# Two phases of a kernel in one program block: each engine goes on by single waits where all engines met

## The reference, cut to what matters

```
# phase A: layer norm, RWKV attention (16 heads, chunks), output projection, residual
out = rwkv(layernorm(x)) + x                     # x1
# phase B: layer norm, mixture of experts, residual
router_logits = h @ gate_w.T                     # h = layernorm(x1), 8 experts, 2 chosen per token
capacity = int(s * K / E * CAP_FACTOR)           # 320 rows at most for each expert and batch item
h1, h3 = dispatch @ w1[e], dispatch @ w3[e]      # 256 -> 896
expert_out = (silu(h1) * h3) @ w2[e]             # 896 -> 256
final = sum over chosen experts of prob * expert_out
```

## Time and profile before

| | us |
|---|---|
| median of 3 executions | 925.23 |
| lowest, highest | 925.21, 929.25 |
| the profiled execution | 925.3 |
| its span, first to last instruction | 923.2 |

### The profile page before, as it was taken

One profiled execution on the slowest core, in us unless ns is written; L12 is line 12 of the kernel. 1 busy time (PEld: TensorE's weight loads), 2 busy tenths in 40 slices (PEclk: granted clock), 3 DMA queues, 4 the chain that ended last, 5 costly groups with the idle time before them and its releaser, 6 DMA issues. The chain is left out here.

```text
span 923.2 us, 19140 instructions
## 1 busy us (share of the span) xinstructions
PE 851.7 (92%) x6919; PEld 724.0 (78%) x6920; DVE 490.8 (53%) x1207; ACT 462.5 (50%) x844; POOL 454.3 (49%) x496
## 2 busy tenths in 40 slices
PE   3999899999999999697999999999799999999995
PEld 2778777777777777687889889879689879889885
DVE  5887788888888876233442342442142343242330
ACT  3567666666666767154443452443253444353331
POOL 5445666666555666356237346237236136437024
PEclk9999999999999999799999999999899999999998
DMA  4840222212111122456024417025325214414113
GB/s 149 330 167 24 88 89 68 67 54 77 37 37 37 37 66 77 147 127 167 8 80 86 112 55 138 7 81 87 73 81 86 71 41 105 94 40 46 13 17 42
DMA packets 50470, 74.01 MB, mean 80 GB/s; under 512 B 5056, under 2 KB 42176, under 8 KB 50368
## 3 DMA queue, kind: packets, MB, share of 16 engines
q1 hardware_dynamic: 35488, 53.46, 17.7%
q0 software_dynamic: 14592, 19.18, 12.1%
q10 hardware_dynamic: 288, 0.01, 0.0%
HBM read 38.41 MB, written 34.22 MB: 79 GB/s over the span
## 5 line engine op out<-in xcount | busy, mean ns | idle before, releaser
L1540 POOL TENSOR_TENSOR wlo<-wraw,whi 128x448 fp32r<-128x448 f32 x84 | 102.6, 1225 | 213.3 <-ACT whi L1596 213.3
L1817 PE MATMUL p<-xh,whi 128*128 128x512 f32 (+1 forms) x504 | 191.7, 380 | 13.6 <-PEq L1446 5.6
L1733 DVE TENSOR_TENSOR hid<-gated,p 128x512 f32<-128x512 f32 (+1 forms) x126 | 81.1, 644 | 214.0 <-ACT gated L1610 214.0
L1819 PE MATMUL p<-xh,wlo 128*128 128x512 f32 (+1 forms) x504 | 190.8, 379 | 0.0
L1818 PE MATMUL p<-xl,whi 128*128 128x512 f32 (+1 forms) x504 | 190.4, 378 | 0.0
L1548 POOL DMA_INDIRECT out<-ysb,index x80 | 125.7, 1571 | 95.1 <-ACT ysb L1632 65.0
L1610 ACT ACTIVATE gated<-p 128x512 f32<-128x512 f32 (+1 forms) x126 | 71.0, 564 | 188.6 <-PE p L1819 188.6
L1837 PE MATMUL py<-whi,hh 128*128 128x256 f32 x469 | 135.6, 289 | 10.6 <-PEq L398 7.5
L1839 PE MATMUL py<-whi,hl 128*128 128x256 f32 x469 | 133.0, 284 | 0.0
L1838 PE MATMUL py<-wlo,hh 128*128 128x256 f32 x469 | 132.8, 283 | 0.0
L1817 PEld LDWEIGHTS p<-xh,whi 128*128 128x128 f32 x504 | 95.4, 189 | 34.3 <-issue 12.1
(11 more groups left out here) (197 smaller groups left out, 1434.1 us busy)
## 6 DMA issues: line engine op xcount, KB each, us to landing
wraw<-in_w SPq DMA_DIRECT2D x24, 896.0 KB
disp<-wraw SPq DMA_DIRECT2D x16, 662.5 KB, 8.8
xtok<-disp SPq DMA_DIRECT2D x16, 530.0 KB, 5.4
x_ring<-in_x SPq DMA_DIRECT2D x16, 256.0 KB, 3.8
out<-x SPq DMA_DIRECT2D x16, 256.0 KB
xtok<-disp SPq DMA_DIRECT2D x8, 265.0 KB, 6.8
out<-ysb,index POOLq DMA_INDIRECT x80
disp<-row,slot_i POOLq DMA_INDIRECT x64
```

Of the source, the lines that this page charges most:

```text
L1540: nc.gpsimd.tensor_tensor(wlo[e.const % 2][m][:, cut], wraw[k][:, cut], whi[e.const % 2][m][:, cut].bitcast(F32), ALU.subtract).then_inc(w ...
L1733: nc.vector.tensor_tensor(hid[k][:, 0:w], gated[k][:, 0:w], p3[k][:, 0:w], ALU.mult).then_inc(hid_ready, 1)
L1817: nc.tensor.matmul(dst[:, 0:w], hi[m][:, wcut], xh[xcut], start=(kt == 0), stop=False)
L1819: ins = nc.tensor.matmul(dst[:, 0:w], lo[m][:, wcut], xh[xcut], start=False, stop=(kt == KT - 1))
```

## The change

Each phase function now returns its five engine programs in place of running them in a block of its own, and `build` puts both in one block, phase A's before phase B's for each engine. Without the meeting, these waits hold what it held: GpSimd waits for the stores of x1 (`x1_out`) before its first add to `out`; TensorE and ScalarE wait for `taken_ready` before their first branch; SP's wait for `sent` before its loads was there already. The `ysb` buffers move to `Kept`, to memory that phase A doesn't use. The PSUM banks of phase B are named in another order, so that the banks of p1 and p3 are those which `early_up` fills, and py0, py1, pt0 and pt1 are banks that phase A is done with. In the diff below, lines that are only shifted to another indentation are left out.

```diff
@@ build @@
-            phase_a(nc, *tensors(ctx), ctx, sem, ident, x, maa, decay_row, decay_ch, u_row,
-                    (wrT, wkT, wvT, wgT, woT), lnw, lnb, gateT, disp, out, whi[0], wlo[0], wraw, expert_views(w1, w3, w2), taken, kept)
+            first = phase_a(nc, *tensors(ctx), ctx, sem, ident, x, maa, decay_row, decay_ch, u_row, (wrT, wkT, wvT, wgT, woT),
+                            lnw, lnb, gateT, disp, out, whi[0], wlo[0], wraw, expert_views(w1, w3, w2), taken, kept)
...
-            phase_b(nc, sb2, ps2, ctx, sem, ident, whi, wlo, wraw, w1, w2, w3, taken, disp, out, kept)
+            second = phase_b(nc, sb2, ps2, ctx, sem, ident, whi, wlo, wraw, w1, w2, w3, taken, disp, out, kept)
+            with nc.Block() as block:
+
+                @block.sync
+                def _(sp):
+                    first[0](sp)
+                    second[0](sp)
...
+                @block.tensor
+                def _(pe):
+                    first[4](pe)
+                    second[4](pe)
@@ class Kept @@
+        self.ysb = [sb(f"ysb{k}", [P, C]) for k in range(NY)]
@@ phase_a @@
-    with nc.Block() as block:
-
-        @block.sync
-        def _(sp):
+    def on_sync(sp):
...
+    return on_sync, on_gpsimd, on_scalar, on_vector, on_tensor
@@ phase_b @@
-    ysb = [sb(f"ysb{k}", [P, C]) for k in range(NY)]
+    ysb = kept.ysb
 
-    p1 = [ps(f"p1_{k}", [P, CW]) for k in range(2)]
-    p3 = [ps(f"p3_{k}", [P, CW]) for k in range(2)]
-    py = [ps(f"py{k}", [P, 512]) for k in range(2)]
-    pt = [ps(f"pt{k}", [P, 512]) for k in range(2)]
+    banks_in_order = {n: ps(n, [P, 512]) for n in ("py0", "p1_1", "p3_1", "p3_0", "pt0", "pt1", "py1", "p1_0")}
+    p1, p3, py, pt = [[banks_in_order[f"{n}{k}"] for k in range(2)] for n in ("p1_", "p3_", "py", "pt")]
...
+    taken_ready, x1_out = sem("taken_ready"), [sem(f"x1_out{k}") for k in range(2)]
@@ phase_b, GpSimd, first @@
             pool.wait_ge(index_early, 1)
+            for k in range(2):
+                pool.wait_ge(x1_out[k], 16 * STEPS // 2)
             early = tile_order(e)[:CHUNKS[EARLY][1]]
@@ phase_b, ScalarE, first @@
             scale_out(e, t0 + n - 1)
+            act.wait_ge(taken_ready, 1)
             rest_where_taken(e)
@@ phase_b, TensorE, first @@
             down(e, t0 + n - 1)
+            pe.wait_ge(taken_ready, 1)
             rest_where_taken(e)
```

More of the change, by code:

```diff
@@ L68 @@
 CW = max(n for _, n in CHUNKS) * P
+NY = 4
 EARLY = 1
@@ new lines, in across, with within @@
+                ins.then_inc(across_done, 1)
+        def within(b, t, g):
+            if 0 <= b < STEPS:
+                c, e = g // 2, g % 2
+                pe.wait_ge(attm_ready[g], TPS * b + t + 1)
+                for d in range(BANDS):
+                    ins = nc.tensor.matmul(pY[d * 2 * N:(d + 1) * 2 * N, c, t * Q:(t + 1) * Q],
+                                           v_pad[:, t, c * BANDS + d, e * 2:(e + 1) * 2, :].rearrange("p a n -> p (a n)"),
+                                           attm[g][:, d, :], start=False, stop=(t == TPS - 1 and g == HGS - 1 and d == BANDS - 1),
+                                           skip_group_check=True)
+                ins.then_inc(intra_done[g], 1)
@@ new lines, in group_sums @@
+        def group_sums(b):
+            if 0 <= b < STEPS:
+                pe.wait_ge(ysq_ready, b + 1)
+                wait(pe, x1_ready, b)
+                if b == 0:
+                    pe.wait_ge(set_pool, 2)
+                heads = blockdiag[:].rearrange("p (h n) -> p h n", n=N)[:, :, 0]
+                for t in range(TPS):
+                    for k in range(KT):
+                        ins = nc.tensor.matmul(p_sums[:, t, k * HPB:(k + 1) * HPB], ysq[:, k, t * Q:(t + 1) * Q], heads,
+                                               start=True, stop=True)
+                ins.then_inc(ssum_done, 1)
@@ new lines, in turn2, with logits @@
+        def turn2(b):
+            if 0 <= b < STEPS:
+                pe.wait_ge(xn2_ready, b + 1)
+                for t in range(TPS):
+                    for c in range(KT):
+                        ins = nc.tensor.transpose(p_x2[:, c, t * Q:(t + 1) * Q], row[b % 2][:, t, c * P:(c + 1) * P], ident[:])
+                ins.then_inc(x2t_done, 1)
+        def logits(b):
+            if 0 <= b < STEPS:
+                pe.wait_ge(x2T_ready, b + 1)
+                for t in range(TPS):
+                    for c in range(KT):
+                        ins = nc.tensor.matmul(p_logit[:, t, :], x2T[:, c, t * Q:(t + 1) * Q], gate_sb[:, c, :],
+                                               start=(c == 0), stop=(c == KT - 1))
+                ins.then_inc(logit_done, 1)
@@ new lines, in count @@
+        def count(b):
+            if 0 <= b < STEPS:
+                r = b % 2
+                n = TPS + (b % SPB == SPB - 1)
+                pe.wait_ge(took_ready, b + 1)
+                nc.tensor.matmul(pS[:, 1, 0, 0, 0:n * E], ones[:], before[r][:, 0:n, :].rearrange("p t e -> p (t e)"), start=True, stop=False)
+                nc.tensor.matmul(pS[:, 1, 0, 0, 0:TPS * E], tri[:], took[r][:].rearrange("p t e -> p (t e)"),
+                                 start=False, stop=True).then_inc(count_done, 1)
@@ new lines, in early_turn, with early_up @@
+        def early_turn(i):
+            pe.wait_ge(rows_in, 16)
+            if i == 0:
+                pe.wait_ge(state_ready, TPS * STEPS - 1)
+            else:
+                pe.wait_ge(gT_ready, STEPS)
+            for a in range(CHUNKS[EARLY][1]):
+                ins = nc.tensor.transpose(early_turned[i][:, a * P:(a + 1) * P],
+                                          kept.xtok[:, EARLY_T.start + a, i * P:(i + 1) * P], ident[:])
+            ins.then_inc(turned, 1)
+        def early_up(f):
+            if f == 0:
+                pe.wait_ge(xl_ready, KT)
+                pe.wait_ge(wlo_ready, 2 * WP)
+                pe.wait_ge(attm_ready[HGS - 1], TPS * STEPS)
+                pe.wait_ge(y_ready, STEPS)
+                pe.wait_ge(ysq_ready, STEPS)
+            wait(pe, hid_ready, f - 1)
+            for m, dst in ((0, early_p1[f % 2]), (1, early_p3[f % 2])):
+                for kt in range(KT):
+                    wcut = slice(kt * F + f * P, kt * F + (f + 1) * P)
+                    nc.tensor.matmul(dst, whi[m][:, wcut], kept.xh[:, kt, early_cols], start=(kt == 0), stop=False)
+                    nc.tensor.matmul(dst, whi[m][:, wcut], kept.xl[:, kt, early_cols], start=False, stop=False)
+                    ins = nc.tensor.matmul(dst, wlo[m][:, wcut], kept.xh[:, kt, early_cols], start=False, stop=(kt == KT - 1))
+            ins.then_inc(h_done, 1)
@@ new lines, in on_tensor @@
+        for c in range(-1, TAIL):
+            group_sums(c - 1)
+            across(c, 0)
+            scores_a(c)
+            outer(c)
+            turn1(c + 1)
+            project_g(c)
+            spread(c - 1)
+            within(c, 0, 0)
+            scores_b(c)
+            within(c, 0, 1)
+            within(c, 0, 2)
+            across(c, 1)
+            within(c, 0, 3)
+            project_r(c + 1)
+            project_k(c + 1)
+            for g in range(HGS):
+                within(c, 1, g)
+            count(c - 3)
+            turn2(c - 2)
+            project_o(c - 1)
+            logits(c - 2)
+            project_v(c + 1)
+            turn_k(c + 1)
@@ new lines, in on_tensor @@
+        group_sums(14)
+        across(15, 0)
+        scores_a(15)
+        outer(15)
+        project_g(15)
+        spread(14)
+        within(15, 0, 0)
+        scores_b(15)
+        within(15, 0, 1)
+        within(15, 0, 2)
+        across(15, 1)
+        within(15, 0, 3)
+        within(15, 1, 0)
+        within(15, 1, 1)
+        within(15, 1, 2)
+        within(15, 1, 3)
+        count(12)
+        early_turn(0)
+        early_turn(1)
+        turn2(13)
+        project_o(14)
+        logits(13)
@@ new lines, in on_sync, with load_rows, load_weights, step @@
+    def on_sync(sp):
+        def load_rows(e):
+            e.wait(sp, turned, TB)
+            e.wait(sp, rows_used, 2)
+            for k, (t0, n) in enumerate(ROW_LOADS):
+                if e.reg is None and e.const == 0 and k == 0:
+                    continue
+                src = (t0 - REST) % ST
+                sp.dma_start(xtok[:, t0:t0 + n, :], row_of(rows_view, e)[:, src:src + n, :]).then_inc(rows_in[k], 16)
+        def load_weights(e, m):
+            even, u = pair(e)
+            k = (3 * u + m) % 2
+            e.wait(sp, wlo_ready, 3 * WP, WP * (m - 1))
+            dst = wraw[k][:].rearrange("p (k f) -> p k f", k=KT if m < 2 else FT)
+            sp.dma_start(dst, row_of(w_view[m], e)).then_inc(w_in[k], 16)
+        for k in range(2):
+            sp.wait_ge(sent[k], 16 * TPS * 2 * STEPS // 2)
+        load_rows(At(0))
+        def step(e):
+            nxt = e + 1
+            if nxt.valid(E):
+                for m in range(2):
+                    load_weights(nxt, m)
+                load_rows(nxt)
```

(2 more changed lines are left out.)

2310 lines of the change are left out of this document (1085 added, 1225 removed).

## The result

The changed kernel takes 921.08 us in the median of 13 executions (918.99 to 927.49), the kernel before 926.13 us in 13 (925.21 to 929.77). The ratio is 0.9948, with a 95% interval of 0.9933 to 0.9964: 4.8 us less on 926, between 3.3 and 6.2. Measured again, on two other occasions, it was 0.9960 (0.9943 to 0.9977) and 0.9953 (0.9939 to 0.9967). The direction is clear; the size is at the 0.5% that I had called the line between faster and the same: the median is 0.5 us above that line, 920.6, and 0.08 us above the 921 beyond which I had called the forecast wrong as a whole.

A forecast was written before the change was run, and what follows sets the result against it. TensorE, busy 92% of the span, was taken as the bound, its wait at the phase join the largest reachable. 4.69 (earlier restart) + 1.06 (clock) = 5.75 us off 925.3 gave 919.5 us, range 917.0 to 924.5.

The forecast's parts named there:

- the forecast's own case: At the join, the clock falls and comes back soon, costing 0.8 to 2.7 us: 919.5 us, chance 0.47.
- the sign of 921: Whole program: the forecast is wrong as a whole if the median lies above 921 us.
- Step 1: At the join, TensorE restarts at 378.70 in place of 383.39, after VectorE's last hidden part: gain 4.69 us.
- Step 2: Behind the join, the clock falls once more, costing 1.5 us in place of 2.56: gain 1.06 us.
- Step 3: Behind the removed meeting, the waits put in its place are hidden and cost nothing.
- (a): At the join, SP's wait for `sent` ends 2.3 us behind the last scatter; rows land at 384.3, before TensorE's transposes.
- (b) to (e): Second phase: waits for `x1_out` and `taken_ready`, weight loads and casts, new banks and `ysb` place each cost nothing.
- The signs: Timeline checks: `down` 2.8 us behind `early_up`, released by `hl`; low clock behind; times from fourth tile 5.8 us earlier.
- Clock stays high: At the join, the clock does not fall: gain 7.25 us, 918.0 us; chance 0.26.
- No earlier start: At the join, TensorE gets little or no earlier start: 921 to 926 us; chance 0.16.
- One more stall at a branch: At a branch behind the join, moved code adds 5.0 us and 2.7 of low clock: 927.2 us; chance 0.07.

The follow-up runs named there:

- the late split: Changed kernel with the first two tiles of expert 0's last chunk begun early on the parts of hidden that are there; 918.55 us, 0.9899 to the kernel before.
- the filled kernels: Changed kernel plus 12 unused matmuls on TensorE filling the idle 2.8 us at the join; 922.03 us (0.9942), then 920.97 us (0.9936) to the kernel before.
- two blocks: Changed kernel with two blocks and the meeting between them restored, its other parts kept; 905.6 us, 1.0002 to the kernel before.

## Why the prediction was right, and where not

The forecast of 919.5 us lay 1.6 us below the median of 921.08, and the range, 917.0 to 924.5, held it. The narrower range of the forecast's own case, 918.8 to 920.8, did not, nor did the sign of 921. Some 0.8 us of the miss is the start: the kernel before took 926.13 us over 13 executions and not 925.3. The rest is a gain of 5.05 us in place of 5.75, and the term that was mis-sized is the clock. By its steps:

**Step 1, the meeting goes (4.69 us).** Right, and to a tenth. The idle time was 7.49, 7.50 us in the two traces with the meeting and 2.79, 2.78, 2.79 us in the three of the changed kernel: 4.7 us. The releaser is `hl`, as forecast. The drain and the meeting were told apart by two kernels: with GpSimd's drain alone all is lost (1.0005), with the meeting alone nothing is (0.9948). I had read this from the drains' ends, and it is now shown.

**Step 2, the clock (gain 1.06 us).** That the clock would fall once more was right, in every trace: all of the nine with an idle join, long or short. What it costs was mis-sized. I took 1.5 us; by the 63 matmuls less 7.43 us it was 2.9, 1.7 and 1.7 in the three traces of the changed kernel, and 2.9, 2.9 and 1.7 in those with the late split, with the loop written out, and with the meeting, which have much the same join. Mean: 2.3 us; three of the six lie above the 2.7 that I had called the most. (With the clock up the same matmuls took 7.57 us in the filled kernels and not 7.43, so each of these costs, before and after, is 0.14 us too high.) And the cost of before, which I took from its one trace as 2.56 us, is not fixed either: 1.6 us with two blocks, 1.9 with the drain put back, mean of the three 2.0. So the clock gave nothing, -0.3 us by these means and +1.06 in my sum. 4.7 - 0.3 = 4.4 us agrees with the three measurements (4.8, 3.6, 4.4); each is uncertain by 1.3 us or more. That the sum came as near as it did is in part luck: the term that it had wrong is small beside step 1 and smaller than this uncertainty.

**Step 3.** (a) Right: SyncE goes on 1.85 us behind the last scatter (2.3 expected), and the rows are on the chip 5.0 us before the transposes begin in this trace; even with the join's idle time used up (0.2 us to spare) they are not waited for. (b) to (e) Right: no releaser of that kind appears, and two blocks with the same additions measure 1.0002.

**The signs.** The idle time, its releaser and the low clock came as said. That every time from the fourth tile on would be that of before less 5.8 us did not: the first trace has 2.9 us less there and then next to nothing, for the low clock at 417.9. My first reading of the page was wrong in one point: three of the 40 slices stand below full tenths, not one; beside the seventeenth they are the 29th, with the turn of the loop, and the last. Nothing in the sum hung on it.

**The rivals.** *Clock stays high*: in no trace of an idle join. The row that spoke for it, the idle stretch of 3.11 us, was itself the exception: in the eleven traces that have this stretch, the way from `up` of expert 0 to that of expert 1 took 36.8 us twice, with the clock at 1.00, and 38.3 to 39.5 us nine times, with the clock at 0.50 to 0.72 in the 6 us behind the stretch. One trace shows what happened once; a clock that falls in most executions can't be read from it. *No earlier start*: wrong, the releaser is `hl`. *One more stall at a branch*: none came; the turn of the loop costs 5.4 to 6.4 us in the traces with the loop, about as before, and the kernel with the loop written out shows that the turn is its place. Whether a fetch of instructions is what it waits for, no run shows. The Trainium skill (Runtime: NRT & Kernel Launch, Instruction fetch mechanics) says that code in sequence is fetched ahead, its cost mostly hidden, and that a taken branch out of the pages held waits for a fetch. Both observations agree with it: no wait at the join and none in the written-out code, 5.4 to 6.4 us at the turn.

What stays open: why GpSimd's drain goes on after its transfers are over, why phase A ended 1.5 us later in the first trace after, and the exact worth of the filled join, whose 1.7 us lie within the uncertainty. They are about the 2.1 us that the mean low clock costs against the 7.57 us at full clock.

## What to carry to other kernels

When engines meet, look at the end of each one's drain and not at the meeting: here a meeting without GpSimd's drain cost 0.12 us, and that drain, behind indirect DMAs, made up 4.35 of the 4.7 us; the semaphores of those DMAs, waited for only where their data is used, came at least 3.4 us earlier. An idle stretch of 3 us on a busy TensorE cost nearly twice its length in most traces of this kernel, since another 1.5 to 3 us went to the low clock behind it; fill it with work that waits for its inputs piece by piece. Compare changes of half a per cent stage by stage and over many executions, since one execution's clock moved the time by as much as the change did.

## What the runs showed of the hardware that I had not expected

GpSimd's drain took 8.996, 9.006 and 9.006 us in three traces on two chips, each time begun 3.7 us before the last scatter was over and over 5.3 us behind it. Taken alone it looks like a fixed time, but the three begin at the same point of the same work. The drain at the end of the program has another length. In the trace of before:

```profile
914.66 1.55 POOL L1548 DMA_INDIRECT out<-ysb,index  x1 [0.94 <-ACT ysb L1632]
...
L1488 POOLq DRAIN  x1: 4266/4266/4266, 918.7 to 918.7; - x1
```

It begins 2.5 us behind the last add, when GpSimd has already waited for all adds to land, and still takes 4.3 us (4.4 in the traces of the changed kernel), with no DMA traffic in it. The drains at the join fit this: the traffic is over at 378.6, 358.7 and 361.2, by windows of 0.2 us, and they end at 383.0, 363.0 and 365.6, 4.3 to 4.4 us later. So in all of these traces the drain went on for 4.3 to 4.4 us when no bytes moved any more. What it does in that time, no run shows.

The same program took 905.7 us on one chip and 926 to 927 on others. The difference, 20 us, is in phase A: with the meeting, `down` starts at 363.48 in place of 383.39. A window in the middle of phase A, first on the slower chip (the kernel before), then on the faster (two blocks):

```profile
160.00:180.00 20.00, 18.23 (x229) 14.73 (x229) 16.08 (x50) 13.27 (x22) 12.45 (x19) 1.00 0.16 50
```

```profile
160.00:180.00 20.00, 20.00 (x276) 16.29 (x273) 17.43 (x59) 14.82 (x27) 14.02 (x19) 1.00 0.19 61
```

TensorE is idle for 9% of it on the slower chip and never on the faster, at the same clock. What makes the difference wasn't tried. It is four times what the change is worth, so only runs on one chip can be compared.
